# The depthwise convolution of a hybrid network on VectorE in place of TensorE, in a kernel whose gathers run on GpSimd

## The reference

```
xp = x @ w_in + b_in
h  = depthwise_conv3x3(x, dw_w) + dw_b          # each channel by itself, padding 1
h  = gelu((h - bn_m) * bn_g / sqrt(bn_v + 1e-5) + bn_b)
offset = (h @ w_off + b_off)                    # 4 groups, 9 taps, 2 coordinates
mask   = softmax(h @ w_msk + b_msk)             # over the 9 taps
y  = sum over taps of mask * bilinear(xp, position + tap + offset) @ w_out + b_out
x  = x + gamma1 * layer_norm(y);  x = x + gamma2 * layer_norm(mlp(x))
```

## Time and profile before

| what | value |
|---|---|
| median of 3 runs | 15282.85 us (15266.24 to 15287.42) |
| the profiled execution's own time | 15399.26 us |
| its span, first to last instruction | 15397.4 us |
| mean granted TensorE clock | 0.697 of full speed |
| PE, matmuls | 7675.1 us busy, 50% |
| PE, weight loads | 3859.4 us, 25% |
| DVE | 5935.6 us, 39% |
| ACT | 6773.1 us, 44% |
| POOL | 6700.8 us, 44% |

### The profile page before, as it was taken

One profiled execution on the slowest core, in us unless ns is written; L12 is line 12 of the kernel. 1 busy time (PEld: TensorE's weight loads), 2 busy tenths in 40 slices (PEclk: granted clock), 3 DMA queues, 4 the chain that ended last, 5 costly groups with the idle time before them and its releaser, 6 DMA issues.

```text
span 15397.4 us, 152662 instructions
## 1 busy us (share of the span) xinstructions
PE 7675.1 (50%) x45913; PEld 3859.4 (25%) x45913; DVE 5935.6 (39%) x17381; ACT 6773.1 (44%) x8210; POOL 6700.8 (44%) x7060
## 2 busy tenths in 40 slices
PE   3344554455534555445554455444654445544467
PEld 2122222222222222222222222222222222222234
DVE  3333334333343334333334333443333433343343
ACT  1234642455424554245533455334553355523455
POOL 4444444444444344444444444444444444444430
PEclk6566776677766776667766777666776677766778
DMA  2111111111111111111111111111111111212324
GB/s 61 45 46 34 31 42 44 45 33 34 40 46 41 31 36 42 47 39 32 38 40 46 39 32 37 43 46 37 31 40 41 48 35 33 57 55 62 94 69 158
DMA packets 453794, 711.94 MB, mean 46 GB/s; under 512 B 146561, under 2 KB 260994, under 8 KB 451330
## 3 DMA queue, kind: packets, MB, share of 16 engines
q0 software_dynamic: 225792, 462.87, 11.3%
q1 hardware_dynamic: 227170, 239.11, 4.9%
HBM read 595.45 MB, written 105.96 MB: 46 GB/s over the span
## 4 chain that ended last, share of the span: by engine, by line
another core or an unknown queue 36%; ACT 16%; PE 16%; issue 14%; DVE 12%; DVEq 5%; DMA 1%; SPq 0%; POOL 0%; ACTq 0%; POOLq 0%
ACT tanh L1677 13%; PE score_ps L1846 7%; DVEq L1208 5%; DVE pool_mem L1372 2%; PE value_ps L1875 2%; DVE newton L1243 2%; PE side_ps L1777 1%; DVE rstd L1245 1%; PE turn_ps L1746 1%; PE chain_ps L1814 1%; ACT expo L1687 1%; DVE bst L1250 1%; ACT L1687 1%; PE chain_ps L1822 1%
## 5 line engine op out<-in xcount | busy, mean ns | idle before, releaser
L1677 ACT ACTIVATE tanh<-key_rep,query 128x896 f32<-128x896 f32 (+7 forms) x6400 | 5560.0, 950 | 5834.7 <-remote 3382.9
L1189 POOL DMA_INDIRECT pool_mem<-patches_even,pool_mem x3528 | 3350.3, 950 | 4142.1 <-DVE y L1375 3038.2
L1189 POOL DMA_INDIRECT pool_mem<-patches_odd,pool_mem x3528 | 3350.3, 950 | 4124.9 <-DVE y L1375 3100.9
L1846 PE MATMUL score_ps<-tanh,score_w 128*32 128x512 f32 (+3 forms) x24320 | 3703.9, 650 | 2566.8 <-ACT tanh L1677 1562.2
L1846 PEld LDWEIGHTS score_ps<-tanh,score_w 128*32 128x32 f32 x24320 | 855.6, 126 | 4803.6 <-issue 2891.3
L1875 PE MATMUL value_ps<-values,expoT 128*128 128x129 f32 (+1 forms) x5200 | 1019.9, 346 | 301.0 <-issue 194.6
L1372 DVE TENSOR_TENSOR pool_mem<-pool_mem 128x384 f32<-128x384 f32 x2352 | 1136.1, 552 | 47.7 <-issue 45.5
L1375 DVE TENSOR_REDUCE y<-pool_mem 128x64 f32<-128x2304 f32 x392 | 1000.9, 2553 | 36.0 <-issue 6.7
L1875 PEld LDWEIGHTS value_ps<-values,expoT 128*128 128x128 f32 (+1 forms) x5200 | 898.6, 249 | 423.2 <-issue 300.9
L1441 DVE COPY expoT<-turn_ps 128x512 f32<-128x512 f32 (+4 forms) x800 | 456.9, 572 | 1214.5 <-remote 829.0
L1746 PE MATMUL turn_ps<-ident,expo 128*128 128x128 f32 (+1 forms) x2632 | 572.9, 341 | 682.6 <-DVE expoT L1441 510.4
(11 more groups left out here) (170 smaller groups left out, 6557.5 us busy)
## 6 DMA issues: line engine op xcount, KB each, us to landing
pool_mem<-in_weight SPq DMA_DIRECT2D x64, 1024.0 KB, 9.1
pool_mem<-patches_even,pool_mem POOLq DMA_INDIRECT x3528
pool_mem<-patches_odd,pool_mem POOLq DMA_INDIRECT x3528
patches_even<-pool_mem SPq DMA_DIRECT2D x104, 256.0 KB, 2.0
patches_odd<-pool_mem SPq DMA_DIRECT2D x104, 256.0 KB
pool_mem<-in_x SPq DMA_DIRECT2D x56, 224.0 KB
x_tok<-in_x SPq DMA_DIRECT2D x192, 64.0 KB
x_d<-x SPq DMA_DIRECT2D x192, 64.0 KB
```

What stands on the lines that cost most here:

```text
L1189: pool.indirect_dma_start(gathered[:, b, j * 4 * CG:(j + 1) * 4 * CG], None, patches_flat[int(odd)], bass.IndirectOffsetOnAxis(ap=index[:, ...
L1677: nc.scalar.activation(tanh[:, ui % TANH_SLOTS, :w], key_rep[:, lo:lo + w], ACT.Tanh, bias=query[:, col:col + 1]).then_inc(tanh_done.sem, 1)
L1846: last = mm(score_ps[32 * col:32 * col + 32, ci % 2, lo:hi], score_w[:, place], tanh[:, ui % TANH_SLOTS, lo:hi], start=place == 0, stop=pl ...
```

## The change

The convolution of a band is computed by DVE: one tensor_scalar and eight scalar_tensor_tensor instructions over 128x448 elements, each reading a shifted view of `x_pad` and (from the second on) the running sum `conv_sum` in SBUF, each followed by a drain. ACT reads `conv_sum` in place of the PSUM bank. PE has no `conv` step any more; the diagonal matrices and their building go, and `side_ps` is read by DVE alone. `LASTS` gives DVE 5.7 us for the step, where it gave PE 9.0, so the whole order is worked out anew. In the front area of `pool_mem` 448 columns are added, and what lies behind moves by that much.

```diff
-FRONT = 10072
+FRONT = 10520
...
-SIDE_READER = {"conv": "act"}
...
-    ... ("pe", "conv"): 9.0,
+    ... ("dve", "conv"): 5.7,
...
-        out["pe", ("image_in", g)] = [at(0, "sp", "image_in", g), at(1, "pe", "conv", NBAND - 1)]
-        out["dve", ("image_in", g)] = [at(0, "pe", "image_in", g)]
+        out["pe", ("image_in", g)] = [at(0, "sp", "image_in", g)]
+        out["dve", ("image_in", g)] = [at(0, "pe", "image_in", g), at(1, "dve", "conv", NBAND - 1)]
...
-        out["pe", ("conv", g)] = [at(0, "dve", "image_in", min(g + 1, NBAND - 1)), used,
+        out["dve", ("conv", g)] = [at(0, "dve", "image_in", min(g + 1, NBAND - 1)), used, before("act", "conv", g, NBAND),
                                   before("pe", "offsets", g, NBAND)]
-        out["act", ("conv", g)] = [at(0, "pe", "conv", g)]
+        out["act", ("conv", g)] = [at(0, "dve", "conv", g)]
...
-            for t in range(TAPS):
-                v.tensor_scalar(taps[:, t], ident[:], dw[:, t:t + 1], None, ALU.mult)
...
+                elif what == "conv":
+                    wait(h_ready, n, i - 1)
+                    total_ = conv_sum.rearrange("p (a b) -> p a b", b=W)
+                    for t in range(TAPS):
+                        dy, dx = divmod(t, 3)
+                        tap = x_pad[:, i * BAND_ROWS + dy:(i + 1) * BAND_ROWS + dy, dx:dx + W]
+                        if t == 0:
+                            v.tensor_scalar(total_, tap, dw[:, t:t + 1], None, ALU.mult)
+                        else:
+                            v.scalar_tensor_tensor(total_, tap, dw[:, t:t + 1], total_, ALU.mult, ALU.add)
+                        last = settle()
+                    last.then_inc(conv_done.sem, 1)
...
-                    nc.scalar.activation(h_band[:], side_ps[:, :BAND], ACT.Gelu, bias=bn[:, 1:2], scale=bn[:, 0:1])\
+                    nc.scalar.activation(h_band[:], conv_sum, ACT.Gelu, bias=bn[:, 1:2], scale=bn[:, 0:1])\
...
-                elif what == "conv":
-                    side_free()
-                    wait(band_copied, n, min(i + 1, NBAND - 1))
-                    for t in range(TAPS):
-                        dy, dx = divmod(t, 3)
-                        last = mm(side_ps[:, :BAND], taps[:, t],
-                                  x_pad[:, i * BAND_ROWS + dy:(i + 1) * BAND_ROWS + dy, dx:dx + W],
-                                  start=t == 0, stop=t == TAPS - 1)
-                    last.then_inc(conv_done.sem, 1)
```

More of the change, by code:

```diff
@@ L190 @@
            "l_w", "l_store", "l_save")
[L191 to L192 removed]
+SIDE = ("image_in", "project_in", "patches", "offsets", "route", "logits") + LATE_SIDE
 FIRST = ("image_in", "project_in", "patches")
 LASTS = {
[L196 removed]
+    ("pe", "image_in"): .7, ("pe", "project_in"): 1.9, ("pe", "patches"): .7, ("dve", "conv"): 5.7, ("pe", "offsets"): 1.8,
     ("pe", "turn"): .35, ("pe", "mix"): 1.2, ("pe", "turn_mid"): .35, ("pe", "hidden"): 1.9, ("pe", "mlp_out"): 1.7,
@@ L459, in simulate @@
                 banks[bank_of[n, step]] = True
-        elif step[0] in SIDE and e == SIDE_READER.get(step[0], "dve"):
+        elif step[0] in SIDE and e == "dve":
             side_free = True
@@ L510, in late_steps @@
     turns, last = ROW_T // 4, len(units) - 1
-    front = [at("dve", "weights", NBAND - 1), at("pe", "conv", NBAND - 1), at("pe", "patches", NPATCH - 1),
+    front = [at("dve", "weights", NBAND - 1), at("dve", "conv", NBAND - 1), at("pe", "patches", NPATCH - 1),
              at("sp", "patches", NPATCH - 1), at("sp", "patches", NPATCH - 2), at("pe", "offsets", NBAND - 1)]
@@ L616, in first_order @@
     todo = [(n, e, s) for (e, s), t in times.items() for n in range(2) if n * period + t < period]
-    read = {(n, s) for n, e, s in todo if e == SIDE_READER.get(s[0], "dve")}
+    read = {(n, s) for n, e, s in todo if e == "dve"}
     def due_of(n, step):
@@ L708, in network @@
         dw = sb("dw", [P, TAPS])
-        early = sb("early", [P, TAPS * C + 2 + C + 2 * PARAMS + PARAMS])
+        early = sb("early", [P, 1040])
         views = Views(early)
-        taps = views.take(TAPS * C).rearrange("p (t c) -> p t c", c=C)
         bn = views.take(2)
@@ L715, in network @@
         b_par = views.take(PARAMS)
+        views_end = views.at
         w_out = sb("w_out", [P, 2, C])
@@ L737, in network @@
         h_band = views.take(BAND)
+        conv_sum = views.take(BAND)
         xy = views.take(BAND_SUBS * SAMPLES * 2).rearrange("p (t s a) -> p t s a", s=SAMPLES, a=2)
@@ L949, in network @@
         schedule = list_schedule()
-        side_uses_of = {age: sum(a == age and step[0] in SIDE and step[0] != "conv"
+        side_uses_of = {age: sum(a == age and step[0] in SIDE
                                  for a, step in order_of("pe", schedule)) for age in (-1, 0, 1)}
-        last_conv_of_period = [(age, step[1]) for age, step in order_of("pe", schedule) if step[0] == "conv"][-1]
         block = ctx.enter_context(nc.Block())
@@ L1208, in settle @@
                 return v.drain()
-            for ln in (band_copied, in_copied, patch_ready, index_ready, mask_shifted, sampled, y_copied, mid_ready,
+            for ln in (conv_done, band_copied, in_copied, patch_ready, index_ready, mask_shifted, sampled, y_copied, mid_ready,
                        mid_copied, norm_ready, norm_copied, keys_copied, masked, exp_copied, x2_ready, ln2_ready,
@@ L1215, in _ @@
             v.memset(x_pad[:], 0.0)
+            v.memset(early[:, views_end:], 0.0)
             v.memset(xp_flat[:], 0.0)
@@ L1277, in task @@
                     wait(band_turned, n, i)
-                    wait(conv_done, n, -1)
                     v.tensor_copy(x_pad[:, rs, 1:W + 1], side_bank(n, name)[:, :BAND].rearrange("p (a b) -> p a b", b=W))\
@@ L1711, in _ @@
             mm = nc.tensor.matmul
-            for ln in (band_turned, in_projected, patch_turned, conv_done, params_done, y_turned, mixed, mid_turned,
+            for ln in (band_turned, in_projected, patch_turned, params_done, y_turned, mixed, mid_turned,
                        hid_done, mlp_done, norm_turned, keys_done, scored, exp_turned, quad_used, ln2_turned,
@@ L1724, in side_free @@
             def side_free():
-                if last_conv:
-                    wait(h_ready, *last_conv.pop())
                 if side_uses or not (isinstance(earlier_uses[-1], int) and earlier_uses[-1] == 0):
```

8 lines of the change are left out of this document (1 added, 7 removed).

## The result

| | before | after |
|---|---|---|
| median of 5 runs | 15287.42 us (15266.24 to 15298.33) | 15374.09 us (15353.18 to 15383.15) |
| ratio of after to before | | 1.0055 [1.0042, 1.0069] |
| the profiled execution | 15399.26 us, clock 0.697 | 15374.09 us, clock 0.683 |

The change made the kernel 0.55% slower, some 87 us, where 37 us less were forecast. The sign is wrong; the time lies in the range. The profiled execution of the kernel before was a long one: against it, after is 25 us *shorter*. The two traces serve for where things lie, and only the ratio for the size. In all that follows one run is left out of the medians: one of six of the kernel called "reductions" took 23,598.62 us, at a granted clock of 0.278.

A forecast was written before the change was run, and what follows sets the result against it. Bound taken: not any engine's work but waits, with PE's answers held while GpSimd's gathers run. Terms -63 - 35 - 10 + 35 + 36 = -37 us gave 15,245 us; own range 15,140 to 15,265, whole range 15,080 to 15,480.

The forecast's parts named there:

- the last section: Prediction's closing tests: a sign change could come from steps unrelated to the convolution; cycle lengths by place would show it.
- held stretch: The 25.7 us from a sample's first gather to the release of PE's delayed answer; work there counts nearly nothing.
- Parts 1 and 2: Nine matmuls off PE: 63 us gained in 42 bands near the gathers' start, 35 us in seven bands in the open stretch.
- Part 3: The start, image 0: convolution moves from PE to DVE and nine diagonal-building instructions go; 10 us gained.
- Part 4: Nine more passes on DVE, 6.2 us a band, mostly hidden in its idle time; one in ten exposed, 35 us lost.
- Part 6: Gathers beside DVE's passes slow by 0.15 us each, counting in full over 49 bands; 36 us lost.
- rival D: DVE's passes lock gathers out, lengthening each held stretch by the passes' 6.2 us: 15,480 us; chance 0.05.
- A: Freeing PE's first 7 us after the gathers start is worth nearly all its length, 210 us: 15,100 us; chance 0.07.
- B: New order puts DVE's passes in the open stretch, 6.2 us a band; 26 exposed bands give 15,370 us; chance 0.28.
- C: Old and new convolution both lie in held stretches and nothing else moves: 15,283 us, within 30 us; chance 0.15.
- E: Without dense matmuls TensorE's clock might start the open stretch at 0.5, costing 84 us: 15,330 us; chance 0.07.
- open stretch: Rest of a cycle until DVE sums the next sample, 12.0 us, three engines 71 to 93% busy; time counts in full.

The follow-up runs named there:

- reductions: Changed kernel with passes 2 to 9 as tensor_reduce with one SBUF input, taps' sum left out: 15398.07 us, 1.0078 to the kernel before.
- old order: Changed kernel's convolution passes on DVE, but steps ordered as in the kernel before: 15260.33 us, 0.9984 to the kernel before; repeated 15231.85 us, 0.9976.
- 3.0: Changed kernel with 3.0 for 5.7 in the duration table for DVE's convolution, so another computed order: 15525.13 us, 1.0088 to the kernel before.
- sixth experiment: old order kernel with GpSimd waiting inside each row of 18 gathers; in slow-state groups one wait 13584.78 us (0.8909), two waits 12223.80 us (0.7942).
- one pass: Changed kernel with one of nine convolution passes, order kept: 15370.60 us, 1.0068 to the kernel before; in a fast-state group 9424.84 us, 1.0003.
- one matmul: Kernel before with one of nine matmuls per convolution, order kept: 15193.89 us, 0.9950 to the kernel before; in a fast-state group 9414.28 us, 0.9993.

## Why the prediction was wrong

**The step that failed is the one without a term.** The sum had six parts, for the convolution and what touches it. The moves of all other steps went in at nothing, though the last section said that a change of sign could come from there and what would show it. It was right in that. They cost 125 to 138 us. The cycle lengths by place, mean over images 1 to 6, of two traces of one order agree within 0.4 us on average (old order with old order, changed with changed). Between the old order (mean of two traces) and the new one (mean of three) they differ by up to 19 us. Over the 49 places of an image the longer cycles add up to 158 us and the shorter ones to 139. That makes an image 18 us longer, 110 us for six images, and 33 us more come in image 0. With eight passes less in the new order the cycles at 45 of the 49 places stay within 1.5 us. Here are three neighbouring cycles, places 35 to 37 of the same image, with no band in them in either order. First the passes in the old order, then the changed kernel (columns as above):

```profile
6836.10:6876.20 40.10, 27.91 (x161) 11.90 (x153) 14.39 (x43) 24.62 (x28) 17.02 (x18) 0.79 0.13 35
6876.20:6918.80 42.60, 18.08 (x119) 9.22 (x119) 16.89 (x53) 24.10 (x24) 17.01 (x18) 0.76 0.12 32
6918.80:6953.10 34.30, 17.00 (x109) 9.71 (x113) 10.84 (x28) 19.70 (x22) 17.05 (x19) 0.65 0.15 38
```

```profile
6941.90:6981.50 39.60, 22.81 (x135) 11.55 (x135) 15.38 (x49) 22.91 (x25) 16.95 (x18) 0.78 0.12 33
6981.50:7004.50 23.00, 10.10 (x59) 5.84 (x58) 10.72 (x27) 8.46 (x9) 17.49 (x19) 0.66 0.21 56
7004.50:7053.30 48.80, 18.58 (x118) 7.92 (x119) 10.61 (x26) 24.64 (x27) 16.98 (x18) 0.67 0.11 28
```

In the changed kernel DVE comes to a sample in time for GpSimd to go straight on, 23.0 us for a cycle; the next takes 48.8. The old order gives 42.6 and 34.3. The three together are 5.6 us shorter in the new order, but ACT's busy time in them is 56.0 us for 68.4: less was done, and it has to be done later. In images 1 to 6 the changed kernel has 7.8 cycles under 26 us an image, the old order 5.7, the kernel before 4.3, and the other cycles are 41.0, 39.7 and 39.6 us long. `list_schedule` knows of no held stretch, so nothing in it steers a new order around them. That such an order comes out better or worse by chance is an inference from this; the two new ones that were measured in the held state (5.7 and 3.0) were both slower. Which of the moved steps lose the most isn't isolated and stays open; the open band isn't it, since at place 17 the old order has its passes 13.0 us before the next gathers too.

**The reading of the held stretch** in the earlier trace rows took PE's part to be done when 25 of 28 matmuls had run. It wasn't: the last ended at 7317.21. Nothing in the sum hangs on it, but what holds the others up is in part PE's own slow issue (sixth experiment).

**Parts 1 and 2, 98 us:** near. Eight of nine matmuls gave 76 us, so nine would give some 85 (62 to 108).

**Part 3, 10 us gained:** wrong. In the changed kernel the first gather starts at 102.8 us, not 74.4: DVE has done the passes of three bands, with the copies between them, and begun a fourth's; in the old order it has done one band's and begun a second's. With one pass it is 83.8. In the old order, with all passes, it is 73.5, so this is the order too. Part of the 33 us of image 0 is this; how much isn't settled.

**Part 4, 35 us lost:** a band is 6.5 us, not 6.2, since a two-input pass took 684 ns and not 618. One band in seven is fully open, in the old order as well. **Part 6, 36 us lost:** gathers beside passes lose 0.24 us, not 0.15, but fewer of them lie beside passes, and the rows of gathers sum to 8,770 us for 8,733, the 36 us of the forecast. That they "count in full" failed: with reductions the rows sum to 8,727 us and the time is the same. Neither part can be seen one by one in the held state. Together, passes in the old order cost 85 - 38 = 47 us, for 71 in parts 4 and 6 (38 is the mean of its gains of 32 and 43). This is a difference of runs in different groups, good to some 30 us. The Trainium skill, "SBUF — State Buffer", section "Who interferes with whom", says that a VectorE instruction with two SBUF inputs contends with a GpSimd instruction that reads SBUF, and that tensor_reduce on trn2 doesn't contend. The traces agree, for gathers that read their indices from SBUF: 1.49 against 1.25 us. No gather was locked out for the length of a pass (rival D).

**So the sum was near for the part that it covered, and the forecast wrong.** -37 us were forecast; with the convolution alone moved, -32 and -43 us were measured. That they agree so well is luck in part: part 3 gained 1 us for 10, parts 1 and 2 some 13 less than forecast, and parts 4 and 6, by the subtraction above, cost some 24 less, which sets that off. The order added 125 to 138. That the whole still lies in the stated range is no merit of the sum.

**The rivals.** A's 210 us aren't there: 85 for all matmuls. B has the sign and nearly the time (15,370), but by another way: passes taken out leave the loss. C's condition, that nothing else moves, is what didn't hold. E: the clock of the open stretch behind the place 43 band was 0.79 to 0.88 before, in images 1 to 6. It is 0.55 to 0.91 here, and 0.50 in five of six in the old order. The mean fell with it, from 0.697 to 0.683 and 0.684. Since the old order has the lower clock too and is faster, and the kernel with one matmul has 0.685 and is 76 us faster, it doesn't decide.

## What to carry to other kernels

When an order is computed, an edit of one step is two edits: the step, and a new order of everything else. Test them apart by moving the step within the old order; here that turned a loss of 0.6% into a gain of 0.2%. And when a page puts a third of the chain on a releaser that it can't name, look for what runs during those waits before you tune anything else, and read there what each engine does, not only the one that waits. Here it was some 5,870 of 15,290 us, against which the edit's 37 were small.

## What the runs showed of the hardware

While a row of GpSimd's indirect DMAs runs, PE can issue one instruction in 0.7 or 1.4 us (7311.3 to 7326.1 in the kernel before), and its answers can reach other engines late, until 2 to 4 us after the last gather ended. A pause in the row, which costs some 2.1 us, lets them through. Whether this happens isn't a property of the kernel: one program took 15,270 to 15,394 us in four groups of runs and 9,420 us in two, with the clock at 0.697 and 0.831. The chip with number 3 had one group of either kind; the others ran on four more chips, one free and three held. What decides it stays open. A DVE instruction of 128x448 fp32 with two SBUF inputs takes 684 ns, with one 450 ns (tensor_scalar) or 620 ns (tensor_reduce).
